# Attentions over the context in parts of two key tiles, with three ring banks and spread maxima

## The reference

```python
x = x + _L0_xattn_ref(_layernorm(x), ctx, ...)       # "latent": context normed, keys rotated, scores clipped to +-11
x = x + _L0_ffn_ref(_layernorm(x), ...)              # "experts": top 1 of 8
x = x + _L1_xattn_ref(_layernorm(x), ctx, ctx, ...)  # "cross": biases, softmax
x = x + _L1_ffn_ref(_layernorm(x), ...)              # "self": self-attention with routed values and outputs
```

## Time and profile before

| | us |
|---|---|
| three runs, median (lowest, highest) | 3422.23 (3415.83, 3430.99) |
| the profiled execution | 3413.58 |
| its span from first to last instruction | 3411.6 |
| latent: first scores to last scores | 56.7 to 1044 |
| experts | about 1100 to 1247 |
| cross: first scores to last scores | 1313.8 to 2583 |
| self | 2625 to 3411.6 |

### The profile page before, as it was taken

How to read it: one execution, slowest core, us unless ns; L and a number is a source line. 1 busy time by engine, 2 the same in 40 slices (tenths; PEclk the granted TensorE clock), 3 DMA queues, 4 the chain that set the end, 5 groups by cost and what they waited for, 6 DMA issues and landing times. The chain is left out here.

```text
span 3411.6 us, 35852 instructions
## 1 busy us (share of the span) xinstructions
PE 2691.2 (79%) x12832; PEld 1495.2 (44%) x12832; DVE 1969.4 (58%) x3274; ACT 1104.6 (32%) x1490; POOL 1076.9 (32%) x731
## 2 busy tenths in 40 slices
PE   4999989989996968888989898989985554546465
PEld 3445445545553745444544454445443332323232
DVE  5765675675664754554454445444452777768775
ACT  3434434444442003333233323332331331223131
POOL 3443443443341002322222222222223143524435
PEclk9999999999997978999999999899997776667676
DMA  3000000000001121000000000000001000000000
GB/s 93 6 1 1 32 1 1 32 1 1 13 1 38 50 76 38 1 1 1 31 1 1 1 32 1 1 1 13 1 1 37 4 13 19 12 16 16 0 19 6
DMA packets 70787, 51.65 MB, mean 15 GB/s; under 512 B 12706, under 2 KB 70626, under 8 KB 70626
## 3 DMA queue, kind: packets, MB, share of 16 engines
q1 hardware_dynamic: 70628, 49.55, 4.8%
HBM read 41.15 MB, written 8.39 MB: 15 GB/s over the span
## 5 line engine op out<-in xcount | busy, mean ns | idle before, releaser
L1496 ACT ACTIVATE cross_probs<-cross_scores 128x1024 f32<-128x1024 f32 x256 | 262.3, 1025 | 575.9 <-PE cross_scores L1747 575.9
L1578 DVE TENSOR_REDUCE cross_part<-cross_ring 128x1 f32<-128x512 f32 x512 | 329.9, 687 | 175.5 <-PE cross_ring L1717 174.8
L1496 ACT ACTIVATE latent_probs<-latent_scores 128x1024 f32<-128x1024 f32 x256 | 262.6, 1026 | 333.6 <-PE latent_scores L1743 327.6
L1417 POOL TENSOR_TENSOR cross_acc_pool<-cross_acc_pool,cross_probs 128x1024 f32<-128x1024 f32 x96 | 227.0, 2364 | 445.6 <-ACT cross_probs L1496 445.5
L1763 PE MATMUL latent_outT<-latent_probs,latent_VN 128*64 128x512 f32 x1024 | 288.8, 644 | 3.0 <-DVE latent_probs L1594 3.0
L1763 PE MATMUL cross_outT<-cross_probs,cross_VN 128*64 128x512 f32 x1024 | 287.2, 641 | 0.0
L1717 PE MATMUL cross_ring<-cross_KH,cross_QH 64*128 64x512 f32 x512 | 192.5, 471 | 119.4 <-DVE cross_part L1578 103.9
L1403 POOL TENSOR_TENSOR latent_KR<-latent_rot 128x256 f32<-128x256 f32 x128 | 131.3, 1026 | 426.3 <-DVE latent_rot L1572 426.3
L1594 DVE TENSOR_SCALAR latent_probs<-latent_probs 128x1024 f32<-128x1024 f32 x256 | 217.2, 849 | 20.4 <-ACT latent_probs L1496 20.3
L1417 POOL TENSOR_TENSOR cross_acc_pool<-cross_probs 128x1024 f32<-128x1024 f32 x32 | 76.2, 2381 | 419.3 <-PE cross_ring L1772 419.3
L1717 PEld LDWEIGHTS cross_ring<-cross_KH,cross_QH 64*128 64x128 f32 x512 | 75.2, 188 | 235.6 <-DVE cross_part L1578 211.4
(11 more groups left out here) (302 smaller groups left out, 6102.6 us busy)
## 6 DMA issues: line engine op xcount, KB each, us to landing
latent_C<-in_ctx_dram SPq DMA_DIRECT2D x4, 1024.0 KB, 7.1
cross_C<-in_ctx_dram SPq DMA_DIRECT2D x4, 1024.0 KB, 7.1
latent_XN<-in_x_dram SPq DMA_DIRECT2D x4, 512.0 KB, 4.5
latent_WRAW<-in_L_xattn_Wkv_dram SPq DMA_DIRECT2D x16, 128.0 KB, 2.4
latent_X<-in_x_dram SPq DMA_DIRECT2D x4, 512.0 KB, 3.6
x_after<-latent_X SPq DMA_DIRECT2D x4, 512.0 KB, 2.9
experts_raw<-in_L_ffn_expert_w_dram SPq DMA_DIRECT2D x1, 2048.0 KB
experts_XN<-x_after SPq DMA_DIRECT2D x4, 512.0 KB, 4.0
```

Of the source, the lines that this page charges most:

```text
L1417: nc.gpsimd.tensor_tensor(acc_pool[:, :, :], first[:, :, :], probs[g % PROBS][:, :, :], ALU.add)\
L1496: nc.scalar.activation(probs[g % PROBS][:, :, :], scores[g % 2][:, :, :], ACT.Exp, scale=SCALE)\
L1578: nc.vector.reduce_max(part[:, qt, h, i:i + 1], bank[:, :], AX.X).then_inc(taken, 1)
```

## The change

- The order. A step has four parts of two tiles. A part is: DMA issues and up to three maxima (`front`), AV of the last two tiles (and, in part 0, "evac"), S of its two tiles, up to three maxima more (`mid`, cross), both clips, both adds, then the units (`tail`), then outputs, norms and weight splits (`late`).
- Three ring banks instead of two, and one `outT` bank instead of two. "evac" is new: ScalarE copies `outT` into OT once the step's values are complete, and "norm" scales OT in place.
- `BY_POOL` is (0, 2, 4, 6) instead of (1, 3, 5, 7) in the latent layer and (0, 2, 4, 5, 6) instead of (0, 1, 3, 5, 6) in the cross layer; the first tile of each list is only read by the second one's add.
- The norm's rounds are cut: "stat" and "rows" of two rows each, "aggr" and "newton", spread over the parts of five steps (latent) or four (cross).
- Waits for constants stand where they are used; WO and bo are loaded last, with a semaphore of their own. In the cross layer's head the maxima stand ahead of fold, shift and V, and K 0 is made a step earlier.

```diff
 RING = ("turn", "fold", "q", "kv", "kT", "K", "V", "max", "shift", "sum", "out")
+BANKS = 3
...
+    steps, parts = B * NP, KT // 2
+    front, mid, tail, late = ([[] for _ in range(steps * parts)] for _ in range(4))
...
+        if s > 0 and latent:
+            put(tail, s, 0, ("kT", s, 1), ("sum", s - 1))
+            put(late, s, 0, ("norm", s - 1))
...
+        if p == 0 and b:
+            for t, d in enumerate((1, 2, 3, 3)):
+                put(late, s, d, ("out", b - 1, t))
+            put(late, s, 3, ("store", b - 1))
...
+            if entering:
+                n = b + 1
+                tail[s * parts] = [("kT", s, 1), turn(n, "c", 0), ("sum", s - 1), turn(n, "c", 1)]
+                put(tail, s, 1, turn(n, "x", 0), ("kv", s + 1, 0), turn(n, "x", 1), ("kv", s + 1, 1))
+                put(tail, s, 2, turn(n, "c", 0, 1), ("q", s + 1), turn(n, "c", 1, 1), ("kT", s + 1, 0))
+                put(tail, s, 3, ("kv", s + 1, 2), ("kv", s + 1, 3))
+            elif more:
+                put(tail, s, 1, ("kv", s + 1, 0), ("kv", s + 1, 1))
+                put(tail, s, 2, ("q", s + 1), ("kT", s + 1, 0))
+                put(tail, s, 3, ("kv", s + 1, 2), ("kv", s + 1, 3))
...
+        if more:
+            put(tail, s, 0, ("K", s + 1, 1), ("q", s + 1))
+            maxima = [("max", s + 1, qt, i, h) for i in range(KT // 4) for qt in range(QT) for h in range(2)]
+            for d, (n, m) in enumerate(((3, 2), (3, 2), (3, 3))):
+                put(front, s, d + 1, *maxima[:n])
+                put(mid, s, d + 1, *maxima[n:n + m])
+                maxima = maxima[n + m:]
         if s > 0:
...
+            put(tail, s, 0, ("sum", s - 1))
+            put(late, s, 0, ("norm", s - 1))
+        group, half = divmod(s + 2, 2)
+        values = []
+        if group < steps // 2:
+            if group * 2 // NP == b:
+                values = [(1, ("V", group, 2 * half)), (3, ("V", group, 2 * half + 1))]
+            elif half == 1:
+                values = [(d, ("V", group, t)) for t, d in enumerate((1, 2, 3, 3))]
...
+        elif s + 2 < steps:
+            put(tail, s, 2, ("K", s + 2, 0))
+        if more:
+            put(tail, s, 3, ("shift", s + 1))
...
+    for n in range(steps * parts):
+        s, d = divmod(n, parts)
+        scores = [("S", s, 2 * d), ("S", s, 2 * d + 1)]
+        behind = [("AV", *divmod(s * KT + 2 * d - 2 + i, KT)) for i in range(2)] if n else []
+        if d == 0 and s:
+            behind.append(("evac", s - 1))
+        clips = [("clip", s, 2 * d + i) for i in range(2)] if latent else []
+        adds = [("add", s, 2 * d + i) for i in range(2)]
+        plan += front[n] + behind + scores + mid[n]
+        plan += clips + adds + tail[n] + late[n]
...
-    BY_POOL = (1, 3, 5, 7) if latent else (0, 1, 3, 5, 6)
+    BY_POOL = (0, 2, 4, 6) if latent else (0, 2, 4, 5, 6)
...
-        outT = [ctx.enter_context(nc.psum_tensor(f"{name}_outT{i}", [P, NQ], fp32)) for i in range(2)]
-        ring = [ctx.enter_context(nc.psum_tensor(f"{name}_ring{i}", [P, 512], fp32)) for i in range(2)]
+        outT = ctx.enter_context(nc.psum_tensor(f"{name}_outT", [P, NQ], fp32))
+        ring = [ctx.enter_context(nc.psum_tensor(f"{name}_ring{i}", [P, 512], fp32)) for i in range(BANKS)]
...
             def constants():
-                constant(WO[:, :, :], weights["Wo"].rearrange("(c p) n -> p c n", p=P))
-                constant(bo[:, :], weights["bo"].rearrange("(a n) -> a n", a=1).broadcast_to([P, D]))
...
+                sp.dma_start(WO[:, :, :], weights["Wo"].rearrange("(c p) n -> p c n", p=P)).then_inc(wo_loaded, 16)
+                sp.dma_start(bo[:, :], weights["bo"].rearrange("(a n) -> a n", a=1).broadcast_to([P, D])).then_inc(wo_loaded, 16)
...
+                elif kind == "evac":
+
+                    s = item[1]
+                    b, p = divmod(s, NP)
+                    act.wait_ge(av_done, tile_no(s + 1, 0))
...
+                    nc.scalar.activation(OT[:, p, :], outT[:, :], ACT.Copy).then_inc(evacuated, 1)
...
         def _(dve):
-            dve.wait_ge(const_made, MADE)
-            dve.wait_ge(const_loaded, 16 * CONSTANTS)
...
-                    nc.vector.scalar_tensor_tensor(out=OT[:, p, :], in0=outT[s % 2][:, :], scalar=-1.0, in1=newt[:, :],
+                    dve.wait_ge(evacuated, s + 1)
+                    nc.vector.scalar_tensor_tensor(out=OT[:, p, :], in0=OT[:, p, :], scalar=-1.0, in1=newt[:, :],
                                                    op0=ALU.mult, op1=ALU.mult).then_inc(normed, 1)
...
         def _(pe):
-            pe.wait_ge(const_made, MADE)
-            pe.wait_ge(const_loaded, 16 * CONSTANTS)
+            pe.wait_ge(const_made, EARLY)
```

310 lines of the change are left out of this document (158 added, 152 removed).

## The result

The changed kernel takes 3192.4 us (median of three runs, 3182.9 to 3203.4) against 3422.2 us: ratio 0.933, 95% interval 0.927 to 0.939. The profiled execution took 3182.9 us (span 3181.1), against 3413.6 (span 3411.6).

A forecast was written before the change was run, and what follows sets the result against it. PE was taken to set the pace in both context attentions. Cross loop -98, heads -24 and latent loop +31 made -91 against the profiled 3413.6 us: forecast 3322, range 3195 to 3390.

The forecast's parts named there:

- Junctions: Both attention loops: fewer borders between values, scores and units on PE; latent minus 58 us, cross 0.8 us a step.
- the maxima: Cross loop: 8.8 us a step of PE waiting on reductions replaced by 1.9 of work and 5.2 of waits.
- the heads: Starts of latent and cross layers: no engine waits for all constants any more; 13 and 11, together minus 24 us.
- the low clock behind nine of them (nine norm rounds) -14: Latent loop: low clock following today's kT waits in nine norm rounds goes away, minus 14 us.
- 3.1 is beyond both, so I take 1.5 each time: Latent loop: each new kT wait is followed by a fall of the clock losing 1.5 us; plus 44 us.
- 3.1 us of waiting in each step: Latent loop: PE asks for kT at 22.2, the last KR addition ends at 25.2; new kT waits plus 90 us.
- the pieces of the norms: Latent loop: the next batch's normalisation, cut into pieces on a full VectorE, costs plus 15 us (between 0 and 31).
- The two small terms: Latent loop: values wait 0.3 us a step for a clip, plus 10; output's wait on normalisation goes, minus 7.
- Rival C: Latent loop: a clip wins over POOL's add; kT waits 1.0, no clock loss, latent -86, total 3205 us; chance 0.13.
- Rival D: Cross loop: waits on banks are larger, so the loop gains half; total 3371 us; chance 0.13.
- the one doubt: Third ring bank: the only open doubt whether the change does what it says; a ring held by its slowest unit.
- A latent loop under 950 us: Sign that the forecast is wrong, with VectorE and POOL falling otherwise in the latent layer.

The follow-up runs named there:

- e1: Changed kernel with values and scores interleaved again within each part instead of two tiles' values, then two tiles' scores: 3232.1 us, ratio 0.947.
- e10: Changed kernel with GpSimd on the latent odd tiles, cross maxima two ahead and three behind in parts 1 and 2, values and scores interleaved: 3132.1 us.
- e7: Changed kernel with the next batch's normalisation put back into whole rounds: 3221.4 us, ratio 0.944.
- e3: Changed kernel with GpSimd adding the latent layer's odd tiles instead of the even ones: 3115.4 us, ratio 0.912.
- e12: Changed kernel, even tiles still on GpSimd, but its latent adds wait for both clips of their part: 3124.0 us, ratio 0.916.
- e5: Changed kernel with two ring banks instead of three, order of the work kept: 3528.0 us, ratio 1.033.
- e4: Changed kernel with both layers' starts put back (WO and bo loaded first, engines wait for all constants): 3209.8 us, ratio 0.940.

## Why the prediction came out as it did

**The direction, and what carried it.** Junctions, the maxima, the heads: each was costed as a gain and each is one. The terms for the pairs that e1 and e10 undo held best: 1.24 us a step, 40 us a loop, against 40 (e1) and 43 (e10) of PE's busy time at full clock in the latent loop, 41 and 36 in the cross loop, 0.14 to 0.17 us for each of the 256 borders. The drain that the Trainium skill names for a change of tiling mode (TensorEngine Tiling (Array Packing), Tiling Modes) is, with the 0.05 us estimated in the prediction, about a third of that.

**The latent loop: the clock, then two kinds of wait.** The forecast had +31 and the trace has -74, and the junctions are not what failed:

| term (us) | forecast | measured | how |
|---|---|---|---|
| PE's matmuls at full clock | -58 | -53 | (841.6 - 18.7) - (908.6 - 32.3) |
| low clock | +30 | -14 | 18.7 - 32.3, by stretches of 10 us |
| waits for kT | +41 | +9 | 58.1 - 49.0 |
| other waits of PE | +18 | -16 | (914.5 - 841.6 - 58.1) - (988.2 - 908.6 - 49.0) |
| loop | +31 | -74 | |

- *Clock (44 us off, the largest).* Two steps failed. The first, "the low clock behind nine of them (nine norm rounds) -14", counted nine falls of 1.5 us where the kernel before has 16: the nine, three of which last twice as long, two more behind kT waits of 2.3 and 2.4, and five behind waits for other things, 32 us in all at 1.7 each. The second, "3.1 is beyond both, so I take 1.5 each time", put 44 us on 29 steps of the changed kernel, which has 11 falls and loses 19. Taking the length of one wait as the rule was the mistake: in the changed kernel waits for kT of 2.73 and 2.74 us (until 158.20, 390.11 and 622.18) are followed by full clock, and waits of 1.86 and 1.88 (824.37, 852.57) by a fall. The two stretches of 10 us around and behind 158.20 are at 1.00:

```profile
151.00:161.00 10.00, 7.07 (x43) 3.30 (x43) 9.52 (x17) 3.78 (x6) 4.20 (x3) 1.00 0.01 2
161.00:171.00 10.00, 9.89 (x65) 5.88 (x62) 8.42 (x13) 4.48 (x7) 3.21 (x3) 1.00 0.00 0
```

- *Waits for kT (32 us off).* The step that failed is the length of the chain from the normalisation to the last KR addition, "3.1 us of waiting in each step". Every link is in the timeline above: clip, GpSimd's add first, the held add, low halves, clips, the held add, rotations, KR held by a clip, kT. From the end of part 2's clips, where VectorE's add starts, to the end of the last KR addition the prediction has 12.6 us (25.2 less 12.6), the trace 11.6 (822.37 + 1.85 less 812.59), and PE asks 9.9 us behind that start (824.37 - 1.86 less 812.59), not 9.6. Link by link, from start to start: add 3.4 against 3.2, low halves 1.4 against 1.2, clips 1.4 against 1.3, add 3.4 against 3.2, rotations and KR 3.0 against 2.7. I had added recorded durations, and instructions in a row overlap in the records: two clips are 1.28 us together and 0.68 each, and the low half at 815.77 starts 0.09 before the add's 3.27 us from 812.59 are over. Such tenths took the wait, a small difference of two long chains, from 3.1 down to 1.86 here and 1.7 in the mean (58.1 us in 34 waits).
- *Other waits and the pieces of the norms (34 us off).* The two small terms held: the values wait 8 us more (+10 forecast), the output's 6.8 us are gone (-7). But for the pieces I took +15 "on a full VectorE", and waits of the kernel before that were no term are gone instead: 10.3 us for the row sum's bank and 6.7 of the sum for GpSimd's add. In the kernel before:

```profile
PE latent_ring L1669 <- DVE latent_newt L1612: 10.3, 3, 3.4
...
PE latent_ring L1772 <- POOL latent_acc_pool L1417: 6.7, 3, 2.5
```

  e7 gives the pieces 27 us of gain, give or take a dozen. That they fit into free time of VectorE, of which the loop still has 145 us, fits this and is not shown.
- *Matmuls (5 us the other way).* The pairs that e1 undoes are 40 of the 53; the pairs of units, forecast at 19, have at most the other 13.

Rival C came nearest with 3205, and that is luck: it let a clip win over GpSimd's add, and in the trace GpSimd's is first in 58 of the 64 parts in which the two adds meet and holds the second clip in 31 more places. "Whoever loses, an add is still held" was said against it; e3 and e12 show why that is no argument: it matters greatly *which* add, since the rotations that kT waits for queue behind VectorE's, and behind GpSimd's add mainly its own sum of the rotated keys. The prediction saw POOL win by 0.25 us; the other way round was worth 63 to 69 us (e12, e3).

**The grouping itself.** Forecast -58 in the latent layer. The 40 us of it that e1 undoes are there as PE's busy time, but in the changed kernel they are worth nothing in the length of the loop that can be told (e1: 11 us less without them), since PE waits at kT for what it saves at the borders; once that wait is gone they are worth 25 (e10). In the cross layer the same pairs, forecast at 40, are worth 45 (e10) to 60 (e1), low clock included.

**The cross loop (26 us off).** The waits stood at the right places and in the right order of size, each a little long: per wait 1.66 against 1.9, 0.26 against 0.5, 1.13 against 1.4, 0.55 against 0.8, 0.45 against 0.6, and not in every step, so 109 us against 5.2 x 32 = 166. Part of the 0.2 to 0.3 us by which each is shorter is how it is read: the forecast counted from when PE has handed in its last matmul, the trace from the modelled end of the record, which for the two maxima at 1708.57 is 0.27 later (0.50 for the pair, 0.23 inside a run). The clock was no term at all, and gave 30 us: low clock costs 49 us before and 19 in the changed kernel. With both, the forecast's own sum would be about -185; the trace has -124.5, so what I took away was overstated by some 60. The norms are 8 of it (e7: 5 for 13). Most of the rest fits the maxima themselves, put at 1.9 us for sixteen without waiting: their recorded busy time is 141 us, 4.4 a step. How much of that is the modelled ends of records was not separated. Rival D, larger waits, falls. What I missed is how much hangs on the third bank: it was called the one doubt, and e5 prices it at 272 us here, 104 of them low clock.

**The heads**: forecast -24, and 39 measured in the two stretches, 27 of it by e4. First statistics at 4.3 us, as "near 5" had it. In the cross layer VectorE idles 7.4 us ahead of its first statistics instead of 18.3.

**The signs given beforehand.** Statistics near 5 us, and 9 or more earlier in the cross layer: yes (4.3; 10.9). Clips' mean above 0.85 and adds towards 2.6: yes (1.00; 2.85 and 1.74). Cross maxima's waits under 102: they are 91 (49.8, 27.2, 6.2, and 8.0 for cross_CTL). A kT line of 90: no, 58. Latent clock below 0.97: no, 0.98. "A latent loop under 950 us" was named as what would prove the forecast wrong, and it is 914.5.

## What to carry to other kernels

Where two engines hold each other, look at which one starts first and at what queues behind each: exchanging two tiles, or adding one wait, moved 63 to 69 us without removing any work. Before putting a price on a fall of the clock, count over the whole loop what it costs in the kernel before; one wait and what followed it is no rule. Cost a chain by the starts of its links in the trace, not by the sum of their durations, all the more where the result is a small difference against another chain. And put no more units in a row ahead of fixed work than there are banks already free; the unit that waits for the slowest bank belongs behind that work.

## What the runs showed of the hardware that was not expected

- The order of the two adds was settled by 0.05 us (e12: 767.19 and 767.24): 1.22 us for VectorE's add with GpSimd's starting behind it, 3.27 the other way, in all 58 cases of the changed kernel. GpSimd's grew from 2.79 (changed kernel) to 3.30 (e3) and 3.43 us (e12).
- The granted clock fell behind waits of 1.86 us (824.40 to 829.50: 0.67), which is less than the 2.28 after which the kernel before ran on at full clock and the 2.73 after which the changed one did (158.20). The length of the last wait does not tell alone; what does was not found out.
- With many waits of up to 2.2 us, none longer, the cross loop of e5 is at 0.91, and its low clock costs 104 us more than that of the changed kernel, nearly as much as the added waits themselves (127 us).
